# Layer 2 attention: the normalising products on DVE as tensor by tensor products with a broadcast reciprocal

## The reference, cut to what matters

```python
q, k, v = x @ Wq, x @ Wk, x @ Wv           # 16 heads of 64
q, k = apply_rope(q), apply_rope(k)
attn = softmax(causal(q @ k.T / sqrt(64)))
x = x + gate * (concat(attn @ v) @ Wo + bo)
```

## Time and profile before

| | |
|---|---|
| median of 3 runs | 1737.76 us (1736.35 to 1740.33) |
| the profiled execution | 1741.61 us, its span in the profile 1739.8 us |
| granted TensorE clock, mean over the span | 0.902 |
| DVE busy | 1116.1 us, 64% |
| L1141, all 192 instructions | 137.4 us busy |
| Layer 2 attention | about 412 to 805 us of the span |

### The profile page before, as it was taken

The page is one execution under the profiler, slowest core; times in us unless marked ns, Lnnn a source line. Parts: engine busy times, 40 slices in busy tenths (PEclk is TensorE's granted clock), DMA queues, the critical chain, the costliest instruction groups (busy, mean ns, idle before and its releaser), DMA issues.

```text
span 1739.8 us, 22228 instructions
## 1 busy us (share of the span) xinstructions
PE 1379.0 (79%) x7062; PEld 861.8 (50%) x7062; DVE 1116.1 (64%) x2431; ACT 933.4 (54%) x2655; POOL 663.9 (38%) x542
## 2 busy tenths in 40 slices
PE   6876004926999999997779999986889968888978
PEld 4422004912555555553346666663666633566643
DVE  2344821324999999995336666646878845778853
ACT  3354001202665666664567777754777743777752
POOL 0010042063655655653001112115767712666730
PEclk7687556966999999999999999988999989999999
DMA  6000102760000000000000000001000000000000
GB/s 247 1 1 0 47 6 82 251 47 5 1 1 1 1 1 1 1 1 1 20 2 4 3 5 5 2 2 72 5 7 3 2 11 1 5 7 3 2 1 24
DMA packets 19265, 38.43 MB, mean 22 GB/s; under 512 B 4020, under 2 KB 12854, under 8 KB 18656
## 3 DMA queue, kind: packets, MB, share of 16 engines
q1 hardware_dynamic: 17120, 34.69, 5.8%
q0 software_dynamic: 2048, 2.54, 2.0%
HBM read 33.07 MB, written 5.77 MB: 22 GB/s over the span
## 4 chain that ended last, share of the span: by engine, by line
DVE 45%; PE 25%; ACT 14%; issue 10%; POOL 4%; DMA 2%; SPq 0%; DVEq 0%; POOLq 0%; ACTq 0%
DVE soft L1141 6%; ACT win_soft L1495 5%; DVE bank L1130 5%; DVE win_q L1579 4%; DVE win_q L1581 3%; DVE rope_part L1121 3%; PE bank L1892 3%; PE bank L1388 2%; DVE win_part L1595 2%; DVE bank L1564 2%; DVE win_neg_max L1567 2%; PE bank L193 2%; ACT win_out L1516 2%; DVE win_sq L1600 2%; ACT win_sq L1472 2%
## 5 line engine op out<-in xcount | busy, mean ns | idle before, releaser
L1669 POOL TENSOR_TENSOR win_soft<-win_soft,win_inv 128x768 f32<-128x768 f32 (+1 forms) x64 | 107.8, 1684 | 335.0 <-DVE win_inv L1605 335.0
L1495 ACT ACTIVATE win_soft<-bank,win_neg_max 128x96 f32<-128x96 f32 (+1 forms) x512 | 173.5, 352 | 82.0 <-DVE win_neg_max L1567 82.0
L1075 ACT ACTIVATE soft<-bank,neg_max 128x512 f32<-128x512 f32 (+3 forms) x256 | 133.3, 535 | 125.3 <-DVE neg_max L1130 124.0
L1141 DVE TENSOR_SCALAR soft<-soft,exp_inv 128x128 f32<-128x128 f32 (+1 forms) x192 | 137.4, 768 | 2.2
L1197 POOL TENSOR_TENSOR rope_part<-rope_part,rope_tab 128x512 f32<-128x512 f32 x64 | 82.2, 1285 | 144.5 <-DVE rope_part L1121 144.5
L1130 DVE CUSTOM_DVE_ANT_0 bank<-bank,att_mask 128x512 f32<-128x512 f32 (+3 forms) x256 | 118.2, 510 | 6.3 <-PE bank L1001 6.3
L1388 PE MATMUL bank<-win_sq,head_sum 128*128 128x512 f32 x192 | 105.5, 637 | 19.8 <-ACT win_sq L1472 17.6
L1653 POOL TENSOR_TENSOR win_part<-win_part,scaled_tab 128x512 f32<-128x512 f32 x64 | 81.6, 1274 | 97.3 <-DVE win_part L1595 97.3
L1371 PE MATMUL bank<-shifted,win_w 128*128 128x512 f32 x128 | 74.5, 669 | 42.9 <-ACT win_v L1508 33.6
L1087 ACT ACTIVATE softT<-bank 128x512 f32<-128x512 f32 x160 | 93.5, 612 | 24.4 <-PE bank L1015 24.4
L1495 ACT ACTIVATION_READ_ACCUMULATOR win_soft<-bank,win_neg_max 128x1 f32 x512 | 104.7, 205 | 0.0
(11 more groups left out here) (303 smaller groups left out, 3458.6 us busy)
## 6 DMA issues: line engine op xcount, KB each, us to landing
moe_w<-in_moe_w SPq DMA_DIRECT2D x8, 960.0 KB, 6.1
y_tok<-in_moe_w SPq DMA_DIRECT2D x8, 960.0 KB, 5.7
wmod<-in_wmod SPq DMA_DIRECT2D x1, 1536.0 KB, 9.1
att_w<-in_att_w SPq DMA_DIRECT2D x1, 1536.0 KB, 8.7
win_w<-in_local_w SPq DMA_DIRECT2D x8, 192.0 KB, 2.3
xg_dram<-zeros SPq DMA_DIRECT2D x5, 256.0 KB, 9.5
y_dram<-y_slot SPq DMA_DIRECT2D x16, 80.0 KB
x<-in_x SPq DMA_DIRECT2D x4, 256.0 KB, 4.2
```

The lines of the kernel that those rows point to most:

```text
L1075: nc.scalar.activation(soft[par][:, hd, TILE_AT[t]:TILE_AT[t] + keys(t)], score_bank(u, s, hd)[:, at:at + keys(t)], ACT.Exp, scale=-1.0, b ...
L1141: last = nc.vector.tensor_scalar(p, p, exp_inv[:, par, n:n + 1], None, ALU.mult)
L1495: nc.scalar.activation(a["soft"][u % 2][:, j, :], bank[2 + half][:, 128 * k:128 * k + a["keys"]], ACT.Exp, bias=a["neg_max"][:, u % 2, j:j ...
L1669: nc.gpsimd.tensor_tensor(a["soft"][u % 2][:, :, :], a["soft"][u % 2][:, :, :], a["inv"][:, u % 2, :].unsqueeze(2).to_broadcast([128, NBLK ...
```

## The change

The product of a tile by its reciprocal sums, on DVE, is issued as `tensor_tensor`, whose second operand is the column of reciprocals broadcast along the row, in place of `tensor_scalar` with the column as a scalar per partition. Operands, results, order and semaphores stay as they are.

```diff
                     for t in ts:
                         n = stat_at(t, hd)
                         p = soft[par][:, hd, TILE_AT[t]:TILE_AT[t] + keys(t)]
-                        last = nc.vector.tensor_scalar(p, p, exp_inv[:, par, n:n + 1], None, ALU.mult)
+                        last = nc.vector.tensor_tensor(p, p, exp_inv[:, par, n:n + 1].to_broadcast([128, keys(t)]), ALU.mult)
                     return last
```

## The result

The changed kernel took 1767.39 us (median of 4 runs, 1761.44 to 1776.52) against 1737.78 before: a ratio of 1.0173, 95% interval 1.012 to 1.0227. A second series of five runs of the same kernel gave 1762.61 us against 1740.21, a ratio of 1.0127 (1.0104 to 1.015), 22.4 us. The forecast was 1762, and 24.0 us of growth.

A forecast was written before the change was run, and what follows sets the result against it. DVE was taken to bound Layer 2 attention without waits; full beats and turns with POOL add 0.75 us to each of 32 units, 24.0 us, to the 1737.8 us median, giving 1762 us, range 1753 to 1772.

The forecast's parts named there:

- What bounds the stage: Layer 2 attention: DVE never waits, so any change in L1141's cost changes the 11.78 us unit one for one.
- rivals of a faster kernel: L1141 beside POOL: broadcast leaves POOL alone, 1698 us (7%), or DVE keeps its turn, 1712 us (2%).
- The pace: L1141's six products: a full 1.04 ns beat per column instead of half, plus 0.07 us, from start to start.
- The slow stream: L1141 rival: a constant address streams below a column per beat, adding 80 us in all, 1818 us; chance 2%.
- Exclusion both ways: Layer 2 unit: DVE's broadcast product and POOL's instruction each wait for the other; key sum L1202 near 1.54 us, from 1.28.
- The rival of a broadcast that leaves POOL alone: Six products beside POOL's four instructions run undisturbed; a unit loses 1.23 us, 39 us in all, 1698 us; chance 7%.
- the one in which POOL is not held: Layer 2 unit: only DVE waits, POOL keeps its times; 0.21 us more per unit, 1745 us; chance 2%.
- Who gets its turn: Between DVE's products in a unit: POOL, where it asked first, gets in between and runs first.
- The rival in which DVE keeps its turn: DVE goes from product to product without POOL between; head copy 0.8 us early, 1712 us; chance 2%.
- The sum of 0.75 us per unit: One Layer 2 unit: 0.27 + 0.20 + 0.07 + 0.13 for halves behind POOL, 0.08 for the last two products.
- the walk: One unit retraced with full beats and turns, from the 512-column product to the head copy, moved from 609.80 to 610.55.
- 32 units x 0.75: Layer 2 attention: every unit, the last included, grows 0.75 us, making 24.0 us in all.

The follow-up runs named there:

- the run with row totals: Kernel before, with all six scalar products also writing their row's sum to a spare column nobody reads: 1723.95 us, ratio 0.9902.
- the run with a full row: Changed kernel with a full row of an SBUF table as second operand of all six products, not the broadcast reciprocal: 1762.0 us, ratio 1.0113.
- the large two: Kernel before, with only the products of 512 and 384 columns given the broadcast operand: 1754.06 us, ratio 1.0076.
- POOL's products cut: POOL's two products cut to one of four columns: 1728.2 us on the changed kernel (tensor products), 1727.38 on the kernel before (scalar ones).

## Why the prediction was right, step by step

- **What bounds the stage.** DVE, without a wait; confirmed by the chain and the windows after. Every microsecond by which the products grew was a microsecond of the unit. The prediction says the same of every microsecond that they lose, and that holds only for the first 0.44 us: at 11.32 us TensorE becomes the bound, as the run with row totals shows. The forecast did not need that half of the sentence; its rivals of a faster kernel, at 1698 and 1712 us, are priced too low by it. (The first of them also has 1.23 us where 609.80 - 608.54 is 1.26.)
- **The pace,** a full beat per column for a broadcast operand: right, products behind POOL end 0.54 and 0.41 us after it for 512 and 384 columns. The slow stream did not come; the run with a full row shows the same durations. The rule on neighbouring words in the Trainium skill (Vector Engine (DVE) Microarchitecture Reference, section 5.2) has rows for operands that hop, and none for one that stays on its address. By these runs, 1073 ns against 1072 for 512 columns, its penalty does not apply to such an operand.
- **Exclusion both ways.** Right: 1.07, 1.62, 0.92, 1.04, 0.28 and 0.41 us against the forecast of about 1.08, 1.6, 0.9, 1.06, 0.3 and 0.42; the key's sum on POOL 1.54 as forecast. The rival of a broadcast that leaves POOL alone fell with these rows, and the one in which POOL is not held with POOL's 1.54.
- **Who gets its turn.** Right inside the units: POOL comes in between DVE's products. The rival in which DVE keeps its turn fell.
- **The sum of 0.75 us per unit.** Measured 0.72. From the 512-column product to the head copy the walk has 5.13 us and the unit shown has 5.09; no step is off by more than 0.02, and the largest is POOL's 384-column product, which ends 0.68 and not 0.70 behind DVE's.
- **32 units x 0.75.** Here lies the step of the sum that failed: "The last unit has no rotary products beside it; I count it like the others." Its growth is 0.3 and not 0.75 us (below). Of the 31 intervals between head copies 29 grow by 0.70 to 0.77, most of them by 0.72, one by 0.33 and the last, in which no product runs, not at all, which is the 21.3 us of the stage. With the growth of the first two units ahead of the first copy, 1.4 us, it is 22.7 us, against 24.0 forecast.
- **What lies around the stage.** The range had been widened for it by 4 us below and 2 above. The two medians, 1767.4 and 1762.6, lie inside; two of the first four runs lay above it, at 1772.2 and 1776.5, so for single runs the widening was too small. The kernel before, too, ran up to 1749.1 in a later series, beyond the 1740.3 of the runs that the prediction had.
- **How much of the hit is luck.** That 1762 lies within 1 us of the second series is so in part by chance: the growth was forecast 1.6 us too high (24.0 against 22.4), and the median it was added to lay 2.4 us below that of the later series. The first series was 5 us above the forecast. What the traces bear out without luck is the growth of a unit, 0.72 against 0.75 us.

## What to carry to other kernels

Where DVE and POOL work on SBUF at the same time, the price of a DVE form is not its pace alone but whether it excludes POOL's instructions: a form at half the pace that leaves POOL alone beat the fast one here by 16 us, and a form at half the pace that does not cost 22. To price such an edit, lay the two timelines side by side and walk one period with the rule that an instruction waits for the other engine's current one and then takes its full time; that gave each duration of the products within about 0.05 us. And look at what was waiting for DVE before counting a gain: of some 38 us hoped for, 16 came, since TensorE was 0.44 us per unit away. Two engines that need nearly the same time in a unit also make a control hard to read: an edit can move the bound from one to the other and leave the total where it was.

## What the runs showed of the hardware that was not expected

**Who asked first is not who started first.** In the last unit DVE's 512-column product starts 0.04 to 0.05 us before POOL's. In the kernel before, timeline of DVE and POOL:

```profile
794.17 1.37 DVE L1141 TENSOR_SCALAR soft<-soft,exp_inv 128x512 f32<-128x512 f32 x1
795.46 0.98 DVE L1141 TENSOR_SCALAR soft<-soft,exp_inv 128x384 f32<-128x384 f32 x1
...
794.21 2.01 POOL L1211 TENSOR_TENSOR soft<-soft,exp_inv 128x512 f32<-128x512 f32 x2 [7.30 <-DVE exp_inv L1148]
```

In the changed kernel:

```profile
825.45 0.69 DVE L1141 TENSOR_TENSOR soft<-soft,exp_inv 128x512 f32<-128x512 f32 x1
826.06 1.39 DVE L1141 TENSOR_TENSOR soft<-soft,exp_inv 128x384 f32<-128x384 f32 x1
...
825.50 2.65 POOL L1211 TENSOR_TENSOR soft<-soft,exp_inv 128x512 f32<-128x512 f32 x2 [7.51 <-DVE exp_inv L1148]
```

The scalar product, though 0.04 us ahead, loses its turn and lasts 1.37 us; the tensor product, with the same lead, goes first in 0.69 us and POOL waits. It was so in each profile where the two met: the scalar form lost in three (before, only the last two products changed, POOL's products cut), the tensor form won in five (the changed kernel, its repeat, the large two, the full row, POOL's products cut). Each profile has this meeting once. Why the two forms differ was not tried. The last unit, with no rotary product in front and with this turn won, grows by 0.33 us alone: from the 512-column product to the head copy it takes 3.31 us before and 3.64 after (825.45 to 829.09).

**A slower form freed time.** The row total turns the 0.81 us of a 512-column scalar product into 0.75 and the 1.43 of a 384-column one into 0.61. It moves one column per beat in place of two, and no longer waits for POOL.
